# An expert layer's second product in three fp32r terms, with the tile step reordered and fourteen shared tiles ahead of the experts

## The reference

```
x = layernorm(x + attention(x))          # 16 heads of 32
scores = x @ gate_w.T                    # 8 experts, the best 2 of each token, softmax over the two
routed = sum over the two of weight * ((silu(x @ w_gate[e].T) * (x @ w_up[e].T)) @ w_down[e].T)    # hidden 256
shared = (silu(x @ sh_gate.T) * (x @ sh_up.T)) @ sh_down.T                                        # hidden 512
out = layernorm(x + routed + sigmoid(x @ se_gate_w.T) * shared)
```

## Time and profile before

| | us |
|---|---|
| median of 3 runs | 2034.04 (2031.04 to 2038.78) |
| profiled execution, its own time | 2032.41 |
| its span in the trace | 2030.7 |
| first product of expert tile 1 starts | 1465.32 |
| first product of expert tile 70 starts | 1826.38 |

### The profile page before, as it was taken

The page is one execution under the profiler, slowest core; times in us unless marked ns, Lnnn a source line. Parts: engine busy times, 40 slices in busy tenths (PEclk is TensorE's granted clock), DMA queues, the critical chain, the costliest instruction groups (busy, mean ns, idle before and its releaser), DMA issues.

```text
span 2030.7 us, 31316 instructions
## 1 busy us (share of the span) xinstructions
PE 1964.6 (97%) x10048; PEld 1277.1 (63%) x10049; DVE 1347.5 (66%) x2297; ACT 888.3 (44%) x1571; POOL 941.8 (46%) x893
## 2 busy tenths in 40 slices
PE   7999999999999999999999999999999999999997
PEld 5655555755555755555755544677766666667886
DVE  5777776677777577777577776689243444446865
ACT  2366665366665266666266666421111111112322
POOL 3255665455665355665445556649111111115651
PEclk9999999999999999999999999999999999999999
DMA  7313433403441603431603313784833223347752
GB/s 233 74 35 77 100 80 77 158 17 84 97 93 47 178 27 79 100 82 36 193 27 79 70 42 117 266 314 177 313 132 103 98 98 103 103 161 234 223 174 69
DMA packets 103699, 242.11 MB, mean 119 GB/s; under 512 B 25296, under 2 KB 25808, under 8 KB 98576
## 3 DMA queue, kind: packets, MB, share of 16 engines
q1 hardware_dynamic: 92768, 205.06, 33.5%
q0 software_dynamic: 10800, 35.40, 6.3%
HBM read 132.93 MB, written 56.61 MB: 93 GB/s over the span
## 4 chain that ended last, share of the span: by engine, by line
PE 79%; DMA 6%; SPq 5%; POOL 4%; issue 2%; DVE 2%; ACT 1%; another core or an unknown queue 0%; POOLq 0%; ACTq 0%; DVEq 0%
PE ps_gu L1750 16%; PE ps_s L730 11%; PE ps_side L708 11%; PE ps_ctx L741 10%; PE ps_side L682 9%; PE ps_d L1856 6%; PE ps_sum L754 5%; PE ps_d L1750 3%; SPq L366 2%; DMA inv_rows<-inv_few 2%; POOL gu_lo L1697 2%; PE ps_t L1821 2%; POOL gu_part L1695 1%; DMA gu_sb<-wgu 1%; DMA gu_kept<-gu_part 1%
## 5 line engine op out<-in xcount | busy, mean ns | idle before, releaser
L1012 DVE TENSOR_REDUCE max_half<-ps_side 128x1 f32<-128x512 f32 x1024 | 659.2, 683 | 211.8 <-PE ps_side L708 208.6
L708 PE MATMUL ps_side<-kq_stack 96*128 96x512 f32 x1024 | 409.5, 404 | 5.0 <-DVE max_half L1012 2.3
L730 PE MATMUL ps_s<-kq_stack 97*128 97x512 f32 x937 | 392.0, 419 | 7.7 <-ACT probs_first L897 4.4
L730 PEld LDWEIGHTS ps_s<-kq_stack 97*128 97x128 f32 x937 | 177.4, 189 | 163.6 <-issue 85.5
L897 ACT ACTIVATE probs_first<-ps_s 128x512 f32<-128x512 f32 x326 | 187.5, 599 | 100.8 <-PE ps_s L730 84.0
L708 PEld LDWEIGHTS ps_side<-kq_stack 96*128 96x128 f32 x1024 | 195.5, 191 | 57.2 <-DVE max_half L1012 25.6
L897 ACT ACTIVATE probs_mid<-ps_s 128x512 f32<-128x512 f32 x308 | 177.5, 599 | 112.1 <-PE ps_s L730 97.3
L629 POOL TENSOR_TENSOR acc<-probs_first,probs_mid 128x512 f32<-128x512 f32 x129 | 164.2, 1299 | 130.1 <-ACT probs_mid L897 127.9
L897 ACT ACTIVATE probs_last<-ps_s 128x512 f32<-128x512 f32 x303 | 175.8, 599 | 96.7 <-PE ps_s L730 80.8
L629 POOL TENSOR_TENSOR acc<-probs_last,probs_first 128x512 f32<-128x512 f32 x129 | 163.3, 1292 | 116.1 <-ACT probs_first L897 112.9
L1705 POOL DMA_INDIRECT x_g<-x,who_all x71 | 67.3, 948 | 314.7 <-PE ps_t L1821 306.6
(11 more groups left out here) (255 smaller groups left out, 3658.1 us busy)
## 6 DMA issues: line engine op xcount, KB each, us to landing
kq_stack<-kq SPq DMA_DIRECT2D x192, 256.0 KB, 5.2
y_slots<-y_t SPq DMA_DIRECT2D x71, 256.0 KB, 2.3
x_r<-x SPq DMA_DIRECT2D x32, 256.0 KB
x_t<-x SPq DMA_DIRECT2D x32, 256.0 KB
gu_sb<-wgu SPq DMA_DIRECT2D x8, 1024.0 KB, 12.6
gu_kept<-gu_part SPq DMA_DIRECT2D x32, 256.0 KB, 2.4
gu_hi<-gu_kept SPq DMA_DIRECT2D x8, 1024.0 KB, 7.0
out<-gu_sb SPq DMA_DIRECT2D x32, 256.0 KB, 2.7
```

Source lines behind the costliest of these rows:

```text
L708: nc.tensor.matmul(bank, q_stack[par][0:3 * HD, h, t * P:(t + 1) * P], k_stack[par][0:3 * HD, h, half * HALF:(half + 1) * HALF], start=Tru ...
L730: nc.tensor.matmul(out, k_stack[par][0:3 * HD + 1, h, kt * P:(kt + 1) * P], q_stack[par][0:3 * HD + 1, h, half * HALF:(half + 1) * HALF], ...
L1012: nc.vector.reduce_max(max_half[:, u // 2, u % 2:u % 2 + 1], bank, AX.X).then_inc(side_free, 1)
```

## The change

The experts' second weights `wd` (8 experts x 2 parts of 128 x 512) are split like the first: 16 further parts for POOL and SP. The low parts stay in SBUF in the place of the weights (`wd_lo`). The high parts are stored to HBM (`wd_kept`), and for every expert tile POOL reads its expert's number into a register and loads the expert's 512 KB of high parts into one of two buffers (`wd_hi`); 71 such loads. `expert_down` becomes six fp32r matmuls. The hidden values of an expert tile get a high part (ACT, new) and a low part (DVE, in the place of its copy).

The step on PE now reads the numbers of the tile and of the one before first, and its order is `expert_turn_hidden(t - 1)`, `expert_turn(t + 1)`, `expert_up(t)`, `expert_down(t - 1)`. Two tiles are turned ahead of the first step. In POOL's list the gather of the tokens of tile t + 3 stands behind the load of the weights of tile t; the first four gathers stand after part 40.

COVER is 14 in place of 12; SP stores 4 parts a tile in place of 5; the load of `gu_hi` begins in the middle of the last covered tile's first product. The loads of x tiles COVER + 2 and COVER + 3 move behind the experts. A stored tile is combined one step later than before. SUMS_LATER is 3 in place of 1. Some semaphores are merged, and arrays are placed anew in SBUF.

```diff
-SUMS_LATER = 1
+SUMS_LATER = 3
-COVER = 12
+COVER = 14
+GATHER_AFTER = 40
+PARTS = E * C + E * CH
-PARTS_A_TILE = 5
+PARTS_A_TILE = 4
...
     for i in range(TT - COVER):
         made = [(COVER + i - 1, False)] if i else []
-        if i < COVER:
-            made.append((i, True))
+        if 1 <= i <= COVER:
+            made.append((i - 1, True))
...
             def store_part(i):
                 sp.wait_ge(router.st_high, 3 * C + i + 1)
-                sp.dma_start(gu_kept[i // C, :, i % C, :], gu_part[:, i % 2, :].bitcast(F32)).then_inc(part_out[i % 2], 16)
+                to = gu_kept[i // C, :, i % C, :] if i < E * C else wd_kept[(i - E * C) // CH, :, i % CH, :]
+                sp.dma_start(to, gu_part[:, i % 2, :].bitcast(F32)).then_inc(part_out[i % 2], 16)
...
             for i in range(2):
-                sp.wait_ge(part_out[i], 16 * (E * C // 2))
-            sp.wait_ge(router.st_split, 3 * C + E * C)
+                sp.wait_ge(part_out[i], 16 * (PARTS // 2))
+            sp.wait_ge(router.st_split, 3 * C + PARTS)
             sp.wait_ge(shared_kept, 16 * KEPT_PIECES)
-            sp.wait_ge(gu_ready, COVER)
+            sp.wait_ge(half_up, 1)
             sp.sem_inc(passed, 1)
             load_high(0)
+            sp.wait_ge(gu_ready, COVER)
             load_high(1)
...
                 store_slots(t, t % 4)
+                if t == NT - 2:
+                    load_tile(COVER + 2)
+                    load_tile(COVER + 3)
...
+                if i == GATHER_AFTER:
+                    pool.wait_ge(placed, 2)
+                    pool.sem_inc(passed, 1)
+                    for t in range(4):
+                        gather_x(t)
             for t in range(NT):
-                if t >= 4:
-                    pool.wait_ge(et_ready, t - 3)
+                if t < 2:
+                    pool.wait_ge((ht_ready, base_done)[t], COVER)
+                    for i in range(2):
+                        pool.wait_ge(part_out[i], 16 * (PARTS // 2))
+                else:
+                    pool.wait_ge(ey_ready, t - 1)
+                pool.sem_inc(passed, 1)
+                e = pool.value_load(tile_expert[0:1, t:t + 1], min_val=0, max_val=E - 1)
+                nc.gpsimd.dma_start(wd_hi[t % 2][:].bitcast(F32), wd_kept[bass.ds(e, 1)].rearrange("a p c d -> (a p) c d")).then_inc(
+                    wd_hi_in[t % 2], 16)
+                if t and t + 3 < NT:
+                    pool.wait_ge(et_ready, t)
                     pool.sem_inc(passed, 1)
-                nc.gpsimd.indirect_dma_start(
...
+                    gather_x(t + 3)
...
             def expert_down(t, s, e):
                 pe.wait_ge(eht_done, t + 1)
+                pe.wait_ge(eht_low, t + 1)
+                pe.wait_ge(wd_hi_in[s % 2], wd_loads(t, s))
...
                 for c in range(CH):
-                    done = nc.tensor.matmul(ps_d[:, s % 2, :], e_hT[:, s % 2, c, :],
-                                            wd_sb[:, bass.ds(e, 1), c, :].rearrange("p a n -> p (a n)"),
-                                            start=c == 0, stop=c == CH - 1)
+                    low = wd_lo[:, bass.ds(e, 1), c, :].rearrange("p a n -> p (a n)")
+                    done = three(ps_d[:, s % 2, :], (e_hT_hi[:, s % 2, c, :], e_hT_lo[:, s % 2, c, :]),
+                                 (wd_hi[s % 2][:, c, :], low), c, CH - 1)
                 done.then_inc(ey_ready, 1)
...
             def expert_step(t, s):
-                expert_up(t, s, expert_of(t))
-                if not is_last(t):
-                    expert_turn(t + 1, (s + 1) % 4)
+                e = expert_of(t)
                 if not static(t, 1):
-                    expert_down(t - 1, (s - 1) % 4, expert_of(t - 1))
-                expert_turn_hidden(t, s)
+                    e_before = expert_of(t - 1)
+                    expert_turn_hidden(t - 1, (s - 1) % 4)
+                    if not is_last(t):
+                        expert_turn(t + 1, (s + 1) % 4)
+                expert_up(t, s, e)
+                if is_last(t):
+                    turn(COVER)
+                if not static(t, 1):
+                    expert_down(t - 1, (s - 1) % 4, e_before)
...
-            expert_turn(0, 0)
+            for t in range(2):
+                expert_turn(t, t)
             down(COVER - 1)
-            pe.wait_ge(wd_in, 16 * E)
-            pe.wait_ge(router.st_split, 3 * C + E * C)
-            pe.wait_ge(expert_known, 1)
+            pe.wait_ge(router.st_split, 3 * C + PARTS)
+            pe.wait_ge(placed, 1)
...
+            def expert_h_high(t, s):
+                act.wait_ge(eht_ready, t + 1)
+                if not static(t, 2):
+                    act.wait_ge(ey_ready, t - 1)
+                nc.scalar.activation(e_hT_hi[:, s % 2], ps_hts[:, s % 2, 0:H].rearrange("p (c t) -> p c t", c=CH),
+                                     ACT.Copy).then_inc(eht_done, 1)
+
             def expert_step(t, s):
+                if not static(t, 1) and not is_last(t):
+                    expert_x_copy(t + 1, (s + 1) % 4)
                 expert_gate(t, s)
-                if not is_last(t):
-                    expert_x_copy(t + 1, (s + 1) % 4)
+                if is_last(t):
+                    x_high(COVER)
+                expert_h_high(t, s)
...
-            def expert_h_copy(t, s):
-                dve.wait_ge(eht_ready, t + 1)
+            def expert_h_low(t, s):
+                dve.wait_ge(eht_done, t + 1)
...
-                nc.vector.tensor_copy(e_hT[:, s % 2], ps_hts[:, s % 2, 0:H].rearrange("p (c t) -> p c t", c=CH)).then_inc(eht_done, 1)
+                nc.vector.tensor_tensor(e_hT_lo[:, s % 2], ps_hts[:, s % 2, 0:H].rearrange("p (c t) -> p c t", c=CH),
+                                        e_hT_hi[:, s % 2].bitcast(F32), ALU.subtract).then_inc(eht_low, 1)
```

More of the change, by code:

```diff
@@ L1419, in feed_forward_memory @@
     gu_part = sb("gu_part", [P, 2, D], F32R)
+    with nc.sbuf_tensor("wd_hi1", [P, CH, D], F32R) as wd_odd:
+        pass
     x_t = sb("x_t", [P, 4, D])
@@ L1430, in feed_forward_memory @@
     all_ones = sb("all_ones", [P, P])
+    y_t = sb("y_t", [P, 4, D])
     token = sb("token", [P, TT], I32)
+    with nc.sbuf_tensor("e_hT_lo", [P, 2, CH, P], F32R) as e_hT_lo:
+        pass
     col = [sb(f"col{i}", [P, TT]) for i in range(8)]
+    col_i = [sb(f"col_i{i}", [P, 2, TT], I32) for i in range(5)]
     cnt = [sb(f"cnt{i}", [P, E]) for i in range(6)]
     cnt_i = [sb(f"cnt_i{i}", [P, E], I32) for i in range(3)]
-    col_i = [sb(f"col_i{i}", [P, 2, TT], I32) for i in range(5)]
     minus_half = sb("minus_half_c", [P, 1])
@@ L1751, in three, with up @@
                 return done
-            def up(t):
+            def up(t, between=None):
                 pe.wait_ge(t_hi, t + 1)
@@ L1762, in up, with up_high_first @@
                     pe.wait_ge(ehid_done, NT)
-                    up_high_first(t)
+                    up_high_first(t, between)
                     return
-                for k in range(2):
-                    for c in range(C):
-                        done = three(ps_gu[:, k, :], (xT_hi[:, t % 2, c, :], xT_lo[:, t % 2, c, :]),
-                                     (sgu_hi[:, c, k, :], sgu_lo[:, c, k, :]), c, C - 1)
+                by_chunk = t == COVER - 1
+                for k, c in sorted(itertools.product(range(2), range(C)), key=lambda kc: kc[1] if by_chunk else kc[0]):
+                    done = three(ps_gu[:, k, :], (xT_hi[:, t % 2, c, :], xT_lo[:, t % 2, c, :]),
+                                 (sgu_hi[:, c, k, :], sgu_lo[:, c, k, :]), c, C - 1)
+                    if by_chunk and (k, c) == (1, C // 2 - 1):
+                        done.then_inc(half_up, 1)
                 done.then_inc(gu_ready, 1)
-            def up_high_first(t):
+            def up_high_first(t, between):
                 pe.wait_ge(router.st_in[0], 32)
@@ L1972, in _ @@
                 if t == 1:
-                    act.wait_ge(gap_ready, 1)
-                    nc.scalar.activation(col[4][:], col[3][:], ACT.Exp).then_inc(exp_done, 1)
-            expert_x_copy(0, 0)
+                    act.wait_ge(chosen, 1)
+                    nc.scalar.activation(col[4][:], col[3][:], ACT.Exp).then_inc(router.curve_done, 1)
+            for t in range(2):
+                expert_x_copy(t, t)
             expert_pipeline(act, expert_step)
-            x_high(COVER)
             for i in range(TT - COVER):
@@ L2237, in _ @@
                     who()
+            for t in range(2):
+                expert_x_low(t, t)
             finish(COVER - 1)
-            expert_x_low(0, 0)
             expert_pipeline(dve, expert_step)
-            x_low(COVER)
             expert_y_copy(NT - 1, (NT - 1) % 4)
```

121 lines of the change are left out of this document (71 added, 50 removed).

## The result

Median of 8 runs of the changed kernel: 2020.99 us (2017.39 to 2028.92); of 8 runs of the kernel before, taken beside them: 2035.99. The ratio is 0.9941, 95% interval 0.9926 to 0.9956: some 12 us faster, where 33.5 were forecast. The forecast was 1999. The time lies in the range (1983 to 2022), at its far end.

A forecast was written before the change was run, and what follows sets the result against it. PE, busy 97% of the span, was taken as the bound, with an equally long ACT and DVE chain in the old order. Gains 28 + 1 + 0 + 3 + 1.5 = 33.5 us took 2032.4 to 1999; range 1983 to 2022.

The forecast's parts named there:

- The step: Expert tiles: six fp32r products and the new order cut a step from 5.233 to 4.83 us, 28 us over 69 steps.
- The 0.05 taken for the loop: Expert step: allowance for hardware loop and late waits, added to 4.78 us of PE work to give 4.83.
- The load of the high weights, steady state: Each expert tile: the new 512 KB load lands in 5.5 us with 8.3 available, so it is hidden; cost 0.
- Into the experts: Entry to the expert tiles: shorter waits, less the new waits, give 1 us gained; bounds 4 gained, 8 lost.
- Its seam: Last covered gate to first product of expert tile 1: old idle stretches go, 3.7 us gained.
- The wait at step 4: Ahead of expert tile 4: PE waits for all of `gu_hi`, some 3 us.
- rival (c): Cover: POOL and SP pace it, `gu_hi` starts 6 us late, PE waits at step 4; 11 us more, 2010; chance 15%.
- Out of the experts: End of the experts, shared weights loading back: 0 net; bounds 1 gained, 5 lost.
- rival (b): Expert steps: the new 512 KB load lands late, after over 8.3 us; step 5.79, time 2065 us; chance 7%.
- The cover and the row sums: Covered shared tiles: PE's waits for x mostly go, 3 us gained; attention's row sums two slots later, 1.5 gained.
- Rival (a): Expert steps: 0.33 us of register and wait latency shows each step, making it 5.11; time 2019 us; chance 10%.
- (d): Whole kernel: something outside the trace takes the gain, leaving the time within 10 us of before; chance 3%.

The follow-up runs named there:

- the half product: Kernel before with one of the two fp32 products of `expert_down` left out, order unchanged; one run, 2025.84 us beside 2034.03 for the kernel before.
- their experiment: Kernel after with the row sums one slot later, as before the change (SUMS_LATER 1 in place of 3); one run, 2026.32 us.
- Mended: Kernel after with eight steps ahead of the loop, earlier stores of results 0 to 3, and shared weights returned in 512 KB pieces; 2009.34 us, ratio 0.9873.
- the fp32 variant: Kernel after with `expert_down` again as fp32 products, on the high parts alone; 2041.05 us, ratio 1.0042 to the kernel before.

## Why the prediction was wrong, step by step

**The step: right.** 28 us were forecast for 69 steps, (5.233 - 4.795) x 69 = 30.2 were found. The six products take 1.41 where 1.37 stood; the hidden values end at 1641.76 and are needed at 1641.97; no wait for a register shows. The 0.05 taken for the loop was too careful: the step is 0.035 shorter than forecast. That the old order would have gained nothing with a shorter product was shown by the half product (5.184).

**The load of the high weights, steady state: right.** 5.5 us forecast, 4.0 found, at 216 GB/s (217 forecast). By the Trainium skill (DMA: Bandwidth & Descriptors, section Anatomy of one DMA) the estimate was 3.2 us; the trace is 0.8 above it in the steady state and 5.0 above it beside the large loads, of which that formula says nothing.

**Into the experts: the first step that failed.** Its seam was right (3.75 against 3.7: the idle stretches of the earlier trace rows are gone, 0.9 for tile 0's hidden values is new). The wait at step 4 was mis-sized: 3 us taken, 12.5 measured. The prediction let the loads of `gu_hi` begin with the half product at 1461.2, and priced their late start only as a rival. They began 5.7 us late, behind the last part's store. What else is in the 12.5: 4.0 of wait that an early start would have left (3 forecast; 1.5 of them are the time from SP's going on to PE's), 1.1 for tile 2's `wd_hi`, which lands beside those loads, and 1.7 for the clock's fall and what follows. So rival (c) was the case, in mechanism, start (6 us late forecast) and place. It priced this at 11 us over the forecast, and 9.5 over it were found; the total is near in part by luck, since its 5 us for traffic stood where 1.0 of longer wait, 1.1 for `wd_hi` and 1.7 for the clock were. The late start and the wait's place are both shown as causes: moving the wait four tiles on gave 8 us back, and an earlier start shortened it by as much as it was earlier.

**Out of the experts: the second.** 0 taken, bounds 1 gained and 5 lost; 7.9 lost, outside the bounds. The mechanism is rival (b)'s: a load of 512 KB that lands later than 8.3 us after its buffer came free, but at two tiles in place of 69. The prediction had the rows for it: gathers of 256 KB took 6.8 us beside the 1 MB loads. It set them aside, as the steady state was not so busy, and did not ask where the experts end in one that is. Pieces of 512 KB, one a step, took the waits for `wd_hi` away, which shows the cause.

**The cover and the row sums: the third, 1 us or so where 4.5 us were taken.** Of the five profiles without an experiment in them, the cover's means are 121.65 after and 122.9 before, 1.2 us, inside the scatter. The waits for x did go, to between 0 and 1.1 us; but in the second profile of the kernel before they are 0.6 too, not 4.5. What took their place is the wait for the hidden values, behind DVE's sorting (3.3 us in the first profile before and 4.7 in the second, 4.5 to 5.1 in the three after). The failed step is an overlap: one profile's waits for x were priced as if nothing stood beside them.

That something did is seen between the gates. From gate 2 to gate 6 are 46.1 to 47.4 us in all seven profiles whose gates 5 and 6 are under 15 us apart, two of the old cover (46.6, 46.8) among them. Only from gate 8 to 9 are these two longer than those with four parts a tile, 14.4 to 14.5 against 12.7. In those seven the cover's means are 121.0 (five with four parts a tile) and 122.6 (two old), 1.6 us. The row sums (1.5 taken) gained nothing, as the waits of their experiment say.

DVE's and then PE's timeline, and the windows of the kernel after:

```profile
1372.71 2.20 DVE L2277 TENSOR_TENSOR x_g<-y_t 128x1024 f32<-128x1024 f32 x1
...
1375.91 0.67 DVE L2070 TENSOR_TENSOR hid<-act_g,ps_gu 128x512 f32<-128x512 f32 x1
```

```profile
1376.63 0.66 PE L1838 MATMUL ps_hts<-ident,hid 128*128 128x128 f32 x4 [1.86 <-DVE hid L2070]
```

```profile
1370.00:1375.00 5.00, 4.78 (x24) 3.61 (x22) 4.97 (x4) 1.09 (x2) 4.92 (x4) 1.00 0.23 84
1375.00:1380.00 5.00, 3.37 (x23) 3.37 (x23) 3.75 (x6) 0.60 (x1) 4.76 (x6) 0.81 0.69 238
1380.00:1385.00 5.00, 5.00 (x20) 4.61 (x20) 4.96 (x4) 0.00 (x0) 3.47 (x4) 0.51 0.52 183
```

An idle stretch of 1.86 us behind a long DVE instruction, then a granted clock of 0.51, the lower level, and gate 5 to 6 takes 17.98 us in place of 13.2 to 14.8. It happens in the kernel before too (17.97 in its second profile), and in six of all thirteen profiles the two gates are 17.9 us or more apart. These six have their first shared gate before 1324.5 or after 1331.7, the seven others between 1326.4 and 1329.7; what connects the two isn't shown. What sets the first shared gate anywhere between 1323 and 1333 wasn't found either.

**The sum again**, with the sizes found and without the scatter: 30.2 (steps) + 3.75 (seam) - 12.5 (step 4) - 7.9 (end) is 13.6. The cover adds 1.6 at most. The table's last row takes some 2 away: it is 187.7 to 187.8 in the three profiles after, and 186.1 and 184.8 in the two before. Of it 0.9 is one more wait for `wd_hi`, the rest wasn't looked into. Together that is about 13, between the 12 of the ratio and the 15 of the medians (2035.99 - 2020.99). Of the 34 us that the steps and the seam earned, 20 were lost again, at the two places where large loads stand beside the small new one. Mended, these gave back 12 to 14. Rival (a) fell (no step at 5.11), and so did (d).

## What to carry to other kernels

Split a repeated step's gain from its two ends, and price the ends with the landing times that hold there: a prefetch with 8 us of room, hidden in the steady state at 4.0, was late at just those tiles where megabytes were on their way. Where a bulk load follows a chain of small stores, its start is where the last store lands, if that is later than where its buffer comes free. A wait for all the pieces, put at a loop's entry, cost 8 us here that waits for each piece, with the loop begun four tiles later, did not. And a wait that goes is worth only what no other engine's wait takes over at the same place.

## What the runs showed of the hardware

- The same load of 512 KB landed after 4.0 us at 216 GB/s, and after 8.2 (up to 10.3) beside loads of 2 MB. With those cut into pieces of 512 KB it landed after 6.2 at a piece a step, and PE no longer waited for it, and after 7.0 with the pieces closer together, with 2.9 us of waits left.
- An idle stretch of PE of 1.86 us was followed by a granted clock of 0.51 for some microseconds in one execution; in that of the fp32 variant one of 1.84 us at the same place was not (every window of 10 us from 1320 to 1480 at 1.00). Idle time alone didn't say which. Nor did a longer one keep PE at the lower clock for longer: three products of tile 4 had records of 0.63 us or more after 9.72 us of idle time, nine after 4.65 in the kernel with five parts a tile.
- From SP's first instruction behind the last landing of `gu_hi` to PE's first matmul were 1.5 us, in the kernel after (1500.11 to 1501.66) and in the one with five parts (1516.20 to 1517.66). What they consist of isn't shown.
- Two fp32 products of 512 columns cost 1.72 us and six fp32r products 1.41: a ratio of 0.82.
